# A graph network in one kernel: two tile pairs of the second layer start before the first stage ends, and the edge layers transpose as float32r

## The reference

```python
x = layernorm(x + gat(x))        # two attention layers, then a dense product
x = layernorm(x + conv(x))       # L1: weighted sum of h @ weight over edges
x = layernorm(x + painn(x))      # L2: equivariant edge layer
x = layernorm(x + mlp_edges(x))  # L3: relu([x_i, x_j] @ W.T + b), summed by source

# gat: h = x @ W1 (512 -> 1024); attention of each edge (and of a loop at each node);
#      out = relu(sum over edges of alpha * h[src] + b1); the same with W2 (1024 -> 1024);
#      then out @ Wfc + bfc (1024 -> 512)
```

## Time and profile before

| | us |
|---|---|
| three runs | 2251.02, 2253.58, 2253.9; median 2253.58 |
| profiled execution | 2249.59 |
| its span, first to last instruction | 2247.9 |
| PE busy in the span | 2199.6 (98%) |
| VectorE, ScalarE, POOL busy | 1487.8, 1024.2, 937.4 |
| mean granted clock of PE | 0.991 |

### The profile page before, as it was taken

The page is one execution under the profiler, slowest core; times in us unless marked ns, Lnnn a source line. Parts: engine busy times, 40 slices in busy tenths (PEclk is TensorE's granted clock), DMA queues, the critical chain, the costliest instruction groups (busy, mean ns, idle before and its releaser), DMA issues.

```text
span 2247.9 us, 36380 instructions
## 1 busy us (share of the span) xinstructions
PE 2199.6 (98%) x12269; PEld 1888.6 (84%) x12269; DVE 1487.8 (66%) x4615; ACT 1024.2 (46%) x2028; POOL 937.4 (42%) x931
## 2 busy tenths in 40 slices
PE   8999999979999999999999999999999999999997
PEld 6878878858899888888999999988888777888785
DVE  8777878744767856666326666267776777678675
ACT  5982112222366632222224656344434666676454
POOL 2017637745222234376552223013444554753542
PEclk9999999989999999999999999999999999999998
DMA  6434665443476748787225667356667777776442
GB/s 215 148 133 136 161 194 193 150 137 106 138 249 216 275 151 278 254 285 252 84 92 175 221 225 258 108 187 227 218 219 236 252 251 246 246 256 227 164 124 69
DMA packets 192495, 435.82 MB, mean 194 GB/s; under 512 B 45751, under 2 KB 74622, under 8 KB 191774
## 3 DMA queue, kind: packets, MB, share of 16 engines
q1 hardware_dynamic: 127034, 249.08, 32.2%
q0 software_dynamic: 65296, 184.67, 26.3%
HBM read 242.68 MB, written 190.96 MB: 193 GB/s over the span
## 4 chain that ended last, share of the span: by engine, by line
PE 72%; DVE 2%; DMA 1%; ACT 1%; issue 1%; POOL 0%; POOLq 0%; SPq 0%; ACTq 0%; DVEq 0%
PE g_h_ps L2625 7%; PE g_h_ps L2642 7%; PE g_h_ps L2627 7%; PE g_h_ps L2626 7%; PE g_h_ps L2643 6%; PE g_h_ps L2644 6%; PE g_h_ps L2667 6%; PE g_h_ps L2669 5%; PE g_h_ps L2668 5%; PE g_t_ps L80 4%; PE g_h_ps L1783 2%; PE g_h_ps L1785 2%; PE g_h_ps L1784 2%; PE g_sum_ps L1023 1%; PE g_sum_ps L1022 1%
## 5 line engine op out<-in xcount | busy, mean ns | idle before, releaser
L2764 ACT ACTIVATE g_act_t<-g_t_ps,g_b_col 128x256 f32<-128x256 f32 (+1 forms) x488 | 202.0, 466 | 371.9 <-PE g_t_ps L80 371.7
L2642 PE MATMUL g_h_ps<-g_x_hi,held_w_hi 128*128 128x256 f32 x1216 | 352.5, 290 | 0.0
L2643 PE MATMUL g_h_ps<-g_x_lo,held_w_hi 128*128 128x256 f32 x1216 | 344.2, 283 | 0.0
L2644 PE MATMUL g_h_ps<-g_x_hi,held_w_lo 128*128 128x256 f32 x1216 | 344.1, 283 | 0.0
L632 DVE CUSTOM_DVE_ANT_0 g_prod<-g_h_sb,g_a_rows 128x256 f32<-128x256 f32 x632 | 224.3, 419 | 79.7 <-ACT g_h_sb L513 71.9
L2667 PE MATMUL g_h_ps<-fc_w_hi,g_x_hi 128*128 128x512 f32 x632 | 268.8, 425 | 2.1 <-DVE g_x_lo L2943 2.1
L2625 PE MATMUL g_h_ps<-held_w_hi,g_x_hi 128*128 128x512 f32 x656 | 264.0, 402 | 0.0
L2627 PE MATMUL g_h_ps<-held_w_hi,g_x_lo 128*128 128x512 f32 x656 | 257.2, 392 | 0.0
L2626 PE MATMUL g_h_ps<-held_w_lo,g_x_hi 128*128 128x512 f32 x656 | 257.1, 392 | 0.0
L2669 PE MATMUL g_h_ps<-fc_w_hi,g_x_lo 128*128 128x512 f32 x632 | 247.5, 392 | 0.0
L2668 PE MATMUL g_h_ps<-fc_w_lo,g_x_hi 128*128 128x512 f32 x632 | 247.0, 391 | 0.0
(11 more groups left out here) (401 smaller groups left out, 4834.2 us busy)
## 6 DMA issues: line engine op xcount, KB each, us to landing
h<-g_h_sb SPq DMA_DIRECT2D x120, 512.0 KB, 3.6
h<-g_rows_own SPq DMA_DIRECT2D x40, 512.0 KB, 4.8
g_x_in<-in_dram SPq DMA_DIRECT2D x39, 512.0 KB, 3.9
h_cols<-g_h_sb SPq DMA_DIRECT2D x38, 512.0 KB, 4.9
xb_rows<-in_dram SPq DMA_DIRECT2D x19, 1024.0 KB, 6.1
xb<-xb_rows SPq DMA_DIRECT2D x19, 1024.0 KB, 4.4
g_x_in<-h_cols SPq DMA_DIRECT2D x38, 512.0 KB, 7.6
g_x_in<-h SPq DMA_DIRECT2D x21, 512.0 KB, 6.4
```

The source lines that it names most:

```text
L2642: pe.matmul(out, wh, xh, start=(k == 0), stop=False)
L2643: pe.matmul(out, wh, xl, start=False, stop=False)
L2644: last = pe.matmul(out, wl, xh, start=False, stop=(k == KC - 1))
```

## The change

Four tiles without edges (74 to 77 in the permuted order) become the second layer's first two macros. Their rows of the permutation are loaded first, in the first stage; POOL gathers their four tiles there (the first two into buffers of the first stage, the next two into `held.next_x`, which lasts into the second); between tiles 77 and 78 of the first layer PE transposes the first two, ScalarE and VectorE make hi and lo, and behind tile 78 PE does the first two halves of their product. The two PSUM banks with these halves, the identity and the bias columns are held over the barrier. The second stage begins with half 2. The fills of macro 1 lie in halves 2 and 3 of macro 0. The attention vectors are loaded later, and one VectorE step (`find_cuts`) moves from half 3 to half 8. POOL waits for PE's tiles at every fourth scatter instead of every third. `turn`, `turn_x` and `turn_sums` use `turn_whole`, with float32r views of the same buffers.

```diff
+FIRST = 2
+FIRST_TILE = TILES - 1 - 2 * FIRST
 # first stage, POOL
-                    if c % 3 == 0:
-                        pool.wait_ge(tile_done, 4 + PERM_FROM + c // 3)
+                    if c % 4 == 0:
+                        pool.wait_ge(tile_done, 4 + PERM_FROM + c // 4)
...
                 pool.wait_ge(slots_out, 16 * (TILES + 1))
-                pool.dma_start(held.perm[:, :, :], perm_tab.rearrange("(t p) k -> p t k", p=P)).then_inc(perm_in, 16)
+                perm_rows = perm_tab.rearrange("(t p) k -> p t k", p=P)
+                early = slice(FIRST_TILE, FIRST_TILE + 2 * FIRST)
+                pool.dma_start(held.perm[:, early, :], perm_rows[:, early, :]).then_inc(perm_in, 16)
                 pool.wait_ge(perm_in, 16)
+                pool.wait_ge(w2_lo_done, KC2)
+                for q in range(4):
+                    pool.wait_ge(h_stored[q], 16 * len(range(q, FIRST_ROWS // P, 4)))
+                for m, rows in enumerate((first_x, held.next_x)):
+                    for j in range(2):
+                        at = held.perm[:, FIRST_TILE + 2 * m + j, ROW1:ROW1 + 1].bitcast(I32)
+                        pool.indirect_dma_start(rows[:, j, :], None, h_out[0:FIRST_ROWS],
+                                                bass.IndirectOffsetOnAxis(at, 0)).then_inc(first_in[m], 16)
+                for part in (slice(0, FIRST_TILE), slice(FIRST_TILE + 2 * FIRST, TILES)):
+                    pool.dma_start(held.perm[:, part, :], perm_rows[:, part, :]).then_inc(perm_in, 16)
+                pool.wait_ge(first_in[1], 32)
+                pool.wait_ge(perm_in, 48)
 # first stage, PE
-                body(PASSES - 1)
+                products(MACROS - 2, PASSES - 1, 0)
+                pe.wait_ge(first_in[0], 32)
+                for f in range(FILLS):
+                    turn_first(f)          # 4 transpositions each
+                products(MACROS - 1, PASSES - 1, 1)
+                pe.wait_ge(w2_lo_done, KC2)
+                for n in range(2):
+                    first_columns(n)       # 48 products of 256 columns, waiting for each split
 # first stage, ScalarE
+                for j in range(2):
+                    evac(MACROS - 2, PASSES - 1, 0, j)
+                for f in range(FILLS):
+                    relu_first(f)          # 2 activations each
+                evac(MACROS - 1, PASSES - 1, 1, 0)
 # first stage, VectorE
+                splits(MACROS - 1, PASSES - 1, 1)
+                attention(MACROS - 2, PASSES - 1, 0, [0])
+                for f in range(FILLS):
+                    split_first(f)
+                attention(MACROS - 2, PASSES - 1, 0, [1])
+                attention(MACROS - 1, PASSES - 1, 1)
 # second stage
-    order = [*range(EARLY_A), *range(ENDS, ENDS + EARLY_B), *range(EARLY_A, ENDS), *range(ENDS + EARLY_B, TILES)]
+    early_end = ENDS + EARLY_B - 2 * FIRST
+    order = [*range(FIRST_TILE, FIRST_TILE + 2 * FIRST), *range(EARLY_A), *range(ENDS, early_end),
+             *range(EARLY_A, ENDS), *range(early_end, FIRST_TILE), *range(FIRST_TILE + 2 * FIRST, TILES)]
...
+        if m == 0:
+            return [(k, f) for i, k, f in ((2, 2, 0), (2, 6, 1), (3, 2, 2), (3, 6, 3)) if i == h]
...
-                gather(0)
+                gather(FIRST)
                 constants()
-                gather(1)
...
-                for f in range(FILLS):
-                    fill(0, f)
-                for h in range(GH):
+                for h in range(2, GH):
                     products(h)
 # edge layers (turn; turn_x and turn_sums alike)
-            last = pe.transpose(h.t_ps[:, k * P:(k + 1) * P], h.sums[:, k * P:(k + 1) * P], h.ident[:, :])
+            last = turn_whole(pe, h.t_ps[:, k * P:(k + 1) * P], h.sums_whole[:, k * P:(k + 1) * P], h.ident_r[:, :])
```

More of the change, by code:

```diff
@@ L165, in dense_and_prep @@
         node_i = sb("node_i", [P, 2, 2, ET], I32)
+        sb.align(P)
+        first_at = sb.end
         marks = sb("marks", [P, 2, TILES])
@@ L194, in dense_and_prep @@
         hid = sb("hid", [F + 1, EP])
+        hid_end = sb.end
         yr = sb("yr", [P, 7, ET])
@@ L197, in dense_and_prep @@
              for buffer in (row[0], row[1], signs[0]) for n in range(2)]
+        first = Space(nc, "first", first_at)
+        held.first_lo = first("lo", [P, KC2, G], F32R)
+        first_act = Space(nc, "first", first.end)("act", [P, 2, HC])
+        first_x = first("x", [P, 2, HC])
+        held.first_hi = first("hi", [P, KC2, G], F32R)
+        assert first.end <= hid_end
+        held.next_x = Space(nc, "first", held.end)("next_x", [P, 2, HC])
+        held.first_at, held.first_end = first_at, first.end
         h_ps = [ps(f"h_ps{s}", [P, HC]) for s in range(2)]
-        f_ps = [ps(f"f_ps{s}", [P, PER, 4 * F]) for s in range(4)]
+        flat_ps = [held.ps[0][:, :], held.ps[1][:, :], *(ps(f"f_ps{s}", [P, 512])[:, :] for s in range(2))]
+        f_ps = [bank.rearrange("p (t k) -> p t k", t=PER) for bank in flat_ps]
         w_in = [sem(f"g1_w_in{s}") for s in range(2)]
@@ L252, in dense_and_prep @@
         u_stored = sem("filt_u_stored")
+        b_in = sem("first_b_in")
+        first_in = [sem(f"first_in{m}") for m in range(FIRST)]
+        first_turned = sem("first_turned")
+        first_relu = sem("first_relu")
+        first_hi_done = sem("first_hi_done")
+        first_lo_done = sem("first_lo_done")
         CONST = 9
@@ L579, in _, with relu_first @@
                     body(i, 0, 0)
-                body(PASSES - 1, 0, 0)
+                def relu_first(f):
+                    act.wait_ge(first_turned, f + 1)
+                    for c in range(2):
+                        k = 2 * f + c
+                        last = act.activation(first_act[:, c, f * G:(f + 1) * G], flat_ps[f][:, c * G:(c + 1) * G], ACT.Relu,
+                                              bias=held.b_col[:, 0, k:k + 1])
+                    last.then_inc(first_relu, 1)
+                for j in range(2):
+                    evac(MACROS - 2, PASSES - 1, 0, j)
+                act.wait_ge(b_in, 32)
+                for f in range(FILLS):
+                    relu_first(f)
+                evac(MACROS - 1, PASSES - 1, 1, 0)
             @block.vector
@@ L652, in body @@
                     attention(2 * i, i, 0)
-                    if not last and ahead < 2:
+                    if ahead < 2:
                         splits(2 * i + 2, i + 1, 0)
@@ L2044, in node_layers @@
         prod_end = sb.end
[L2045 to L2048, removed]
+        ident_r, ident, b_col = held.ident_r, held.ident, held.b_col
+        h_ps = [*held.ps, ps("h_ps2", [P, 512])]
         t_ps = [ps(f"t_ps{s}", [P, 2, G]) for s in range(2)]
@@ L2067, in node_layers @@
         e.cut = early("cut", [H, EP + 1])[:, :]
-        assert early.end <= fwd_at
+        assert early.end <= min(fwd_at, held.first_at)
         e.fwd = Space(nc, "g2", fwd_at)("fwd", [H, EP])[:, :]
@@ L2275, in loads @@
         def loads(m, j):
-            return len([n for n in range(m + 1) if n % 2 == m % 2 and j < len(units(n)) and by_pool(n) == by_pool(m)])
+            return len([n for n in range(FIRST, m + 1) if n % 2 == m % 2 and j < len(units(n)) and by_pool(n) == by_pool(m)])
         def x1_landed(m):
@@ L2835, in finish_y @@
                     last.then_inc(y_done, 1)
-                for f in range(FILLS):
-                    relu(0, f)
                 def beside(g):
@@ L3089, in _ @@
                 dve.tensor_copy(e.key_col[:, :], tabs[:, :, KEY]).then_inc(key_set, 1)
-                for f in range(FILLS):
-                    split(0, f)
-                dve.wait_ge(a_in, 16)
-                dve.wait_ge(const_done, 3)
+                dve.sem_inc(hi_done, FILLS)
+                dve.sem_inc(lo_done, FILLS)
+                dve.wait_ge(const_done, 1)
                 dve.wait_ge(key_set, 1)
```

130 lines of the change are left out of this document (83 added, 47 removed).

## The result

The changed kernel takes 2235.09 us (median of four runs, 2232.87 to 2238.74) beside 2252.3 (four runs) of the kernel before: ratio 0.9926, 95% interval [0.9913, 0.994], so 17 us faster. Forecast were 2233 in 2227 to 2242. The time is within 2.1 us of the forecast, the gain is not: 20.9 us were worked out, and the interval allows 13.5 to 19.6. The profiled execution took 2232.96 us, with a span of 2231.3: 16.6 less than before.

A forecast was written before the change was run, and what follows sets the result against it. PE bounds the kernel, so time comes only from its instructions or its standing, chiefly the 14.7 us wait at the handover. Handover 15.3 plus float32r 5.6 makes 20.9 us: 2253.6 to 2232.7, said as 2233, range 2227 to 2242.

The forecast's parts named there:

- What is left of the handover: Between the stages: 18.6 us lost today, less 1.7 for the barrier and 1.6 for a stall, gains 15.3 us.
- the new stall: Second pair's transpositions, now in halves 2 and 3, make PE wait for the split: 1.6 us, bounds 0 and 2.5.
- The early gathers: Between tiles 77 and 78: both gathers land by 452.2, PE asks at 456.42, slack 4.2 us, so no cost.
- rival 3: Early gathers late, PE waits between tiles 77 and 78; landing at 485 gives 2261; 3% slower, 2% about even.
- The clock: Behind the barrier: the granted clock stays 1.00 after the short pause; a failed cover would cost up to 4 us.
- POOL's lag: Second stage: POOL's gathers come only 2.3 us earlier, PE 15; slack suffices, cost 0, bounds 0 and 5.
- rival 2: PE stands at half 8 or 12 for a gather, some 4 us in all; 2237 us; 11%.
- Rival 4: Barrier waits for permutation or stores instead of PE, clock low again; 5 to 8 us off, 2240; 6%.
- Transpositions as float32r: Edge layers, 20 tiles: groups save 0.11 (convolution sums), 0.11 (PaiNN sums), 0.06 (node rows); 5.6 us, bounds 0 and 9.
- rival 1: Edge layers: float32r brings nothing, groups being bound by loading weights in either type; 2238 us; 11%.
- All 0: Tile order, later attention-vector load, bias loads moved to the first stage and identity made once: no cost or gain.
- The base: Whole kernel: the time before the change, taken as 2253.6 us, the median of three runs.

The follow-up runs named there:

- e4: Changed kernel with the first pair's 96 early products moved behind the barrier, its gathers, transpositions, Relus and splits still early; 2245.74 us, 0.9977 of the kernel before.
- e6: Changed kernel with the second pair's four transposition groups two k-steps earlier in halves 2 and 3; 2231.46 us, 0.9915 of the kernel before.
- e5: Changed kernel with the whole permutation loaded in one transfer ahead of the early gathers; 2244.73 us, 0.9965 of the kernel before.
- e10: Changed kernel with the second pair's transpositions two k-steps earlier, `turn_x` in plain float32 and the identity at the end of SBUF; 2234.81 us, 0.9938 of the kernel before.
- e1: Changed kernel with all three groups of edge-layer transpositions back at plain float32, early macros kept; 2240.38 us, 0.9944 of the kernel before.
- e7: Kernel before with its second stage's buffers at the changed kernel's addresses, instructions and order unchanged; 2253.19 us, ratio 1.0002.
- e3: Changed kernel with `turn` and `turn_x` back at plain float32, `turn_sums` left as float32r; 2232.11 us, 0.9919 of the kernel before.
- e2: Kernel before with float32r in `turn`, `turn_x` and `turn_sums` and nothing else; 2247.09 us, 0.9985 of the kernel before.

## Why the prediction was right, and where it was not

- **What is left of the handover:** right. 15.3 us forecast, 15.0 measured; e4 shows that it takes both the early chain (5.8 us of the gain stay without the early products) and the cover by the products (9.3). Barrier 1.7 forecast, 1.5 measured; the new stall 1.6 and 1.3, of which e6 brings back 1.1. PE's last early product ends at 474.6 (forecast 474.9).
- **The early gathers** (rival 3): not late. The small load took 3.4 us to land, POOL went on at 443.94 (forecast 445.4), the gathers landed a median of 5.8 behind their issues, so about 451, and PE asked at 456.1. Forecast for the whole load was a wait of 4 us; e5 has 3.4, and 1.6 more from the clock. The Trainium skill's fit (DMA: Bandwidth & Descriptors, Anatomy of one DMA) makes, as an estimate, 2.0 us of these 8 KB and 2.4 of the 158 KB in e5; 3.4 and 11.5 were measured, so it doesn't hold for these two. POOL reached the load 2.2 us earlier than in the kernel before (440.24 against 442.41), where the prediction had no change; whether the new pacing of the scatters did that wasn't tested.
- **The clock:** right in this profile, but the step ("the clock stays 1.00") rested on one pause of nearly 2 us, and e10 shows that such a pause doesn't always leave it there.
- **POOL's lag** (rival 2): costs nothing, as forecast. The attention rows begin at 479.81 (forecast 480.6), and PE is busy for all of 490.70 to 600. VectorE's wait of 4 us didn't come: it starts on the scores at 540.90 with no idle time before them.
- **Rival 4:** didn't happen, but e4 shows the mechanism: without PE's cover the barrier waits for scores and stores, and the clock falls.
- **Transpositions as float32r:** the step that failed. Taken were 0.11, 0.11 and 0.06 per group, 5.6 us; the two profiles gained 2.8 (the prediction named 5 as a sign of being right). The eight profiles with float32r sums have a mean PaiNN stretch of 131.9 (131.5 to 132.6), the three of plain float32 (before, e1, e7) 134.1 (133.9 to 134.5): 2.3 us, which is 0.11 for each of 20 groups of sums, as forecast, and leaves nothing for the node rows: e3 and e10, where these are plain, have 131.7 and 131.8. The 0.11 for the sums is right partly by luck: their group before was read as 0.44 from three transpositions, and is 0.47. In conv the means of seven and four profiles are 439.4 and 439.7: 0.3 instead of 2.2, and no more than single profiles differ. There the group itself got shorter by 0.14, but the fp32 product behind it grew by 0.07, and PE then waited on the split (`conv_t_lo`: 0.9 to 1.3 us in all with float32r, 0.3 to 0.4 without). The prediction's own first figure, 0.08, had the longer product in it but not the wait; it was then raised, "up to 0.15 where the next product hides its weight load", and for that place the runs show the opposite. So rival 1's result, that nothing is gained, came in two of three places, but its reason, groups bound by loading weights, fits the node rows alone: in conv the group did get shorter. The sums went from 0.47 to 0.28. The Trainium skill (TensorE: Matmul & The Clock Gate, Terms) has the transpose mode four times faster for FP32; that float32r then has nothing left to win, as the prediction worked out from it, isn't what these rows show.
- **"All 0" for what is moved:** 1.2 us were lost to new addresses between half 28 and Wfc, a term that the sum didn't have. The later load of the attention vectors and the move of `find_cuts` weren't tested by themselves; no wait of PE in the kernel after is put down to them.
- **The base:** the median of three runs, 2253.6, was high; medians of 4 to 19 runs of the kernel before were 2250.0 to 2252.4. The 20.9 us were too large by 4.3 against the two profiles (2.8 by float32r, 1.2 by addresses, 0.3 at the handover), and the base was too high by 1.3 to 3.6, which hid part of it. So it is partly luck that the time came out within 2.1 us.

Left open: which buffer's address costs the 1.2 us. e7 and e10 have in common that the identity and the bias columns lie elsewhere, and that the macros' buffers lie 512 bytes nearer to the edge buffers; moving either alone wasn't tried. Also open is what spreads the way to t77 over 455 to 463 us. The windows show where e1 loses its 6.1 us against the kernel after: 5 of them between 250 and 310 us, by a wait of 3.1 on a split and a granted clock of 0.97 over these 60 us (1.00 and no wait in the kernel after), the rest from 310 to 360 at 0.97 against 1.00. Why that split comes late isn't shown.

## What to carry to other kernels

A handover between two stages costs the gather, the chain behind it and the slow clock after the pause; starting the next stage's first tiles early pays when there is enough work of the tensor engine to lie over the last stores: here 11.5 us of products were worth 9.3. A shorter instruction is worth what the chain shows together with its neighbour: look at the instruction behind it, and at the wait behind that, before multiplying a saving by a count. And effects of a microsecond in a long kernel are read from the same stretch in several profiles, not from medians.

## What the runs showed of the hardware

- **Granted clock after a pause of PE:** 1.5 us left it at 1.00 in six profiles and gave 0.69 over 5.5 us in one; 3.4 us gave 0.53 over 3.3; 8.1 gave 0.50 over 5.6; 14.7 gave 0.51 over 7.9. A pause can so cost more than its length: by 1.6 us for 3.4, 2.8 for 8.1, and once 1.7 for 1.5.
- **A float32r transposition** of plain columns saves 0.13 to 0.19 us per group of four against float32 (0.43 to 0.30 for conv's sums; 0.47 to 0.28 for PaiNN's, where three of the four have 64 columns), lengthens the next instruction by 0.05 to 0.07, and saves nothing in groups of which three quarters are read with a stride of three (0.46 in both). The strided loads themselves take 194 to 197 ns at the median in either type, those of the same size without a stride 139 to 142.
- **Addresses alone** moved a stretch of 819.2 us (before, e2) to 820.4 (e7), with the same instructions in the same order.
